# First attention: maxima one block of keys further ahead, weighting by the values in two halves

## The chip, the cores and the metric

The kernel runs on one core of one Trainium2 chip. The metric is the device time of one execution in microseconds (us), the median of several runs. The engines are called PE (TensorE, matrix products), DVE (VectorE), ACT (ScalarE), POOL (GpSimd) and SP (SyncE, which issues DMA transfers). PEld is PE's weight load, and an engine's name with a q (SPq) its sequencer.

## The reference

The input x has 2 batches of 2048 tokens with 256 features. Two residual blocks follow one another: an attention over all tokens, and a two-layer network with local attention. The change touches the first alone:

```
def _L0_attn_ref(x, Wq, bq, Wk, bk, Wv, bv, Wo, bo):
    q = _rope(proj(Wq, bq))        # 16 heads of 16 features, 2048 tokens
    k = _rope(proj(Wk, bk))
    v = proj(Wv, bv)
    scores = jnp.einsum('bhtd,bhsd->bhts', q, k) / scale
    attn = jax.nn.softmax(scores, axis=-1)
    out = jnp.einsum('bhts,bhsd->bhtd', attn, v)
    return jnp.einsum('btc,oc->bto', out, Wo) + bo

x = x + _layernorm(_L0_attn_ref(_layernorm(x, axis=-1), ...), axis=-1)
x = x + _layernorm(_L0_ffn_ref(_layernorm(x, axis=-1), ...), axis=-1)
```

## The kernel before

The program runs its phases one after the other: projection to queries, keys and values, `attention_phase`, output projection, feed-forward layers, and a final sum. All engines' orders are written out by hand, in one function per engine, and semaphores join them.

`attention_phase` handles 2 x 16 = 32 heads (NH) of 2048 tokens each. A head has 16 tiles (TB) of 128 tokens and 4 blocks (BLOCKS) of 512. A **step** is one tile of 128 keys of one head against the four blocks of 512 queries, so there are 512 steps. In a step

- PE makes four blocks of scores with `score` (L632), each into one of three banks `scores` (BANKS1). It waits until ACT has emptied the bank, which is done with the block of three blocks before.
- ACT makes the exponential of each block, with `exponentiate` (L696), into one of 12 slots of `probs` (three steps). At a step's first block it waits until PE has weighted the step three before (`pv_done`).
- PE weights the values with `weigh` (L644): four matmuls for the four blocks, each with a stationary operand of 32 columns at its own column position, into one bank `pv`, which accumulates over a head's 16 steps. In the trace each of these matmuls in full float32 has two records, so a call has eight.

The exponentials need each query's maximum over all keys beforehand. PE makes the scores again with queries as the stationary operand, in `for_dve` (L600), on another group of rows of the array than `score`, and DVE takes the maximum of two blocks at once with `take_maximum` (L729). Two blocks are a **unit** and lie in two banks of `aux`, of which there are two pairs; `unit_of` numbers the units. This runs ahead of the scores by AHEAD = 3 spans of 8 tiles, so the maxima of 24 tiles (OPENING) are made in an opening of their own, where ACT (L689) and DVE (L737) share the work. The queue of PE in the main loop is, for each block: `score`, then `for_dve` for the block 24 tiles ahead, and at block 1 of a step `weigh(step - 2)` behind them.

Once in a head the 16 x 128 maxima are transposed by PE (`maximum_rows`, L622, into a unit of `aux`), copied by DVE (`copy_rows`, L743), and sent by SP (`load_rows`, L488) to rows of `q_stack` for the scores of the next head. This sits at slot 13 of a head's second span, which is block 1 of step 11. When a head's weighting is complete, ACT copies `pv` to `o_stage` (`copy_outputs`, L704), at block 2 of the next head's step 1, and the next head's first `weigh` waits for the copy.

SP works through one list for each head n, and begins when PE raises `head_begun`, behind the score of block 1 of step 1: six loads of head n+1 for the scores, six loads of head n+2 for the maxima (both L482, from `qk_dram`), the inverse sums of head n-2, the outputs of head n-1 (L497, L498), the rows of head n+1 (L488), and the sums (L515, L503). The first maxima of a head wait for all six of its loads (`for_max_loaded`); its first score waits for its own six and for the rows.

Of the kernel before, what the change touches and what calls it, by code (L numbers as in the profile page):

```python
# [16 lines left out]
TB = T // P  # L17
# [345 lines left out]
BLOCKS = T // 512  # L363
BODY = 3
VW = 32
SPAN = TB // 2
SLOTS = SPAN * BLOCKS
SPANS = NH * TB // SPAN
AHEAD = 3
OPENING = AHEAD * SPAN  # L370
FIRST_ROWS = TB + 3
ROWS_SLOT = 13
PROBS = 3 * BLOCKS
BANKS1 = 3
LOADS = 6
# [24 lines left out]
def attention_phase(nc, qk_dram, sums_dram, VO, mask_sb, shift_sb, ident, load_output_weights):  # L400

    with ExitStack() as ctx:
# [32 lines left out]

        block = ctx.enter_context(nc.Block())

        WITH_MAXIMA = SPANS - AHEAD
        FIRST_ITEMS = 2 * OPENING
        Q_MINUS_PIECES = ((0, 0, 4), (0, 4, TB), (1, 0, SPAN))  # L440

        def item_of_exp(e):

            return FIRST_ITEMS + e

        def rows_here(p, i):

            return p % 2 == 1 and i == ROWS_SLOT and p // 2 + 1 < NH

        block_at = [divmod(i, BLOCKS) for i in range(SLOTS)]  # L450
        unit_of, rows_unit = {}, {}

        def count_units():

            unit = 0
            for t in range(OPENING):
                if t == FIRST_ROWS:
                    rows_unit[0] = unit
                    unit += 1
                unit_of[t, 0] = unit  # L460
                unit += 1
            for p in range(SPANS):
                for i in range(SLOTS):
                    if p < WITH_MAXIMA and block_at[i][1] % 2 == 1:
                        t, k = block_at[i]
                        unit_of[(p + AHEAD) * SPAN + t, k // 2] = unit
                        unit += 1
                    if rows_here(p, i):
                        assert block_at[i][1] % 2 == 1
                        rows_unit[p // 2 + 1] = unit  # L470
                        unit += 1

        count_units()
# [119 lines left out]
        def _(pe):  # L593
# [12 lines left out]
                    pe.wait_ge(act_emptied, item - BANKS1 + 1)  # L606
                return scores[:, item % BANKS1]

            def for_dve(t, keys):

                unit = unit_of[t, keys // 2]
                if keys % 2 == 0 and unit >= 2:
                    pe.wait_ge(dve_emptied, unit - 1)
                last = score_for_max(t, keys, aux[:, unit % 2, keys % 2])
                if keys % 2 == 1:
                    last.then_inc(dve_filled, 1)

            def maximum_rows(n):
# [13 lines left out]
                last = nc.tensor.matmul(out, k_stack[0:SCORE_ROWS, n % BODY, s * P:(s + 1) * P], q_stack[0:SCORE_ROWS, n % BODY, j * 512:(j + 1) * 512],  # L632
                                        start=True, stop=True).then_inc(act_filled, 1)

            def weigh(step):

                n, s = divmod(step, TB)
                if s == 0:
                    pe.wait_ge(v_made, n + 1)
                    if n:  # L640
                        pe.wait_ge(pv_copied, n)
                pe.wait_ge(act_emptied, item_of_exp(BLOCKS * (step + 1) - 1) + 1)
                for j in range(BLOCKS):
                    last = nc.tensor.matmul(pv[VW * j:VW * (j + 1)], v_ones[:, n % BODY, s, :], probs[:, (BLOCKS * step + j) % PROBS],  # L644
                                            start=(s == 0), stop=(s == TB - 1), skip_group_check=True, tile_position=(0, VW * j))
                last.then_inc(pv_done, 1)

            def first_difference(t, k):

                n, tile = divmod(t, TB)  # L650
                piece = [i for i, (head, start, stop) in enumerate(Q_MINUS_PIECES) if head == n and start <= tile < stop][0]
                pe.wait_ge(q_minus_made, piece + 1)
                pe.wait_ge(for_scores_loaded[n], 16 * LOADS)
                out, rows = for_act(2 * t + k), slice(0, SPLIT_ROWS)
                nc.tensor.matmul(out, q_stack[rows, n, tile * P:(tile + 1) * P], k_stack[rows, n, (2 + k) * 512:(3 + k) * 512], start=True, stop=False)
                for_dve(t, k)
                nc.tensor.matmul(out, q_minus_first[rows, t], k_stack[rows, n, k * 512:(k + 1) * 512], start=False, stop=True).then_inc(act_filled, 1)
                nc.tensor.matmul(pv[:], q_stack[max_rows, n, tile * P:(tile + 1) * P], k_stack[max_rows, n, k * 512:(k + 1) * 512], start=True, stop=True)

# [3 lines left out]
                for k in range(2):  # L663
                    first_difference(t, k)

            for p in range(SPANS):
                for i in range(SLOTS):
                    step, j = p * SPAN + i // BLOCKS, i % BLOCKS
                    score(p * SLOTS + i)
                    if i == 5 and p % 2 == 0:  # L670
                        nc.tensor.nop().then_inc(head_begun, 1)
                    if p < WITH_MAXIMA:
                        for_dve((p + AHEAD) * SPAN + block_at[i][0], block_at[i][1])
                    if rows_here(p, i):
                        maximum_rows(p // 2 + 1)
                    if j == 1 and step >= 2:
                        weigh(step - 2)
            weigh(NH * TB - 2)
            weigh(NH * TB - 1)

        @block.scalar
        def _(act):

            def positive_part(t, k, item):

                act.wait_ge(act_filled, item + 1)
                if t >= 2:
                    act.wait_ge(dve_emptied, unit_of[t - 2, 0] + 1)
                nc.scalar.activation(excess[:, t % 2, k], scores[:, item % BANKS1], ACT.Relu).then_inc(act_emptied, 1)  # L689

            def exponentiate(e):

                act.wait_ge(act_filled, item_of_exp(e) + 1)
                if e >= PROBS and e % BLOCKS == 0:
                    act.wait_ge(pv_done, (e - PROBS) // BLOCKS + 1)
                nc.scalar.activation(probs[:, e % PROBS], scores[:, item_of_exp(e) % BANKS1], ACT.Exp, scale=float(D1) ** -0.5).then_inc(act_emptied, 1)  # L696

            def copy_outputs(n):

                act.wait_ge(pv_done, TB * (n + 1))  # L700
                if n >= 2:
                    act.wait_ge(outputs_moved, 16 * BLOCKS * (n - 1))
                    act.wait_ge(sums_stored, 16 * BLOCKS * (n - 1))
                nc.scalar.copy(o_stage[:, n % 2], pv[:]).then_inc(pv_copied, 1)  # L704

            for t in range(OPENING):
                for k in range(2):
                    positive_part(t, k, 2 * t + k)
            for p in range(SPANS):
                for i in range(SLOTS):  # L710
                    if i == BLOCKS + 2 and p % 2 == 0 and p > 0:
                        copy_outputs(p // 2 - 1)
                    exponentiate(p * SLOTS + i)
            copy_outputs(NH - 1)

        @block.vector
        def _(dve):

            def larger_half(n):

                dve.wait_ge(dve_emptied, unit_of[(n + 1) * TB - 1, 1 if n else 0] + 1)
                nc.vector.tensor_tensor(head_max[:], mx[:, n % BODY, :, 0], mx[:, n % BODY, :, 1], ALU.max).then_inc(head_max_made, 1)  # L722

            def take_maximum(t, half):

                n, tile = divmod(t, TB)
                unit = unit_of[t, half]
                dve.wait_ge(dve_filled, unit + 1)
                nc.vector.tensor_reduce(mx[:, n % BODY, tile, half:half + 1], aux[:, unit % 2].rearrange("p a k -> p (a k)"), AX.X, ALU.max).then_inc(dve_emptied, 1)  # L729

            def take_joined_maximum(t, item):

                n, tile = divmod(t, TB)
                unit, above = unit_of[t, 0], excess[:, t % 2].rearrange("p a k -> p (a k)")
                dve.wait_ge(dve_filled, unit + 1)
                dve.wait_ge(act_emptied, item + 1)
                nc.vector.tensor_tensor_reduce(out=above, in0=aux[:, unit % 2].rearrange("p a k -> p (a k)"), in1=above, scale=1.0, scalar=LOWEST,  # L737
                                               op0=ALU.add, op1=ALU.max, accum_out=mx[:, n % BODY, tile, 0:1]).then_inc(dve_emptied, 1)
# [21 lines left out]
            for t in range(OPENING):  # L760
# [2 lines left out]
                take_joined_maximum(t, 2 * t + 1)  # L763
                if t == TB:
                    larger_half(0)
            for p in range(SPANS):
                n = p // 2
                for i in range(SLOTS):
                    if p < WITH_MAXIMA and block_at[i][1] % 2 == 1:
                        take_maximum((p + AHEAD) * SPAN + block_at[i][0], block_at[i][1] // 2)  # L770
                    if p % 2 == 1 and i == 3 and n + 1 < NH:
                        larger_half(n + 1)
                    if rows_here(p, i):
                        copy_rows(n + 1)
                    if p % 2 == 0 and i == 3 and n >= 2:
                        invert_sums(n - 2)
            invert_sums(NH - 2)
            invert_sums(NH - 1)
# [895 lines left out]
```

## Time and profile before

| | us |
|---|---|
| median of 3 runs | 3165.63 |
| lowest, highest | 3161.74, 3165.71 |
| the profiled execution, its own time | 3163.34 |
| its span in the profile | 3161.5 |
| the exponentials (L696) of attention, in the span | 204.4 to 1571.1 |

The span runs from the first to the last instruction that the profile shows; the execution's own time is 1.8 us longer. Busy time of PE is modelled, since matmuls are pipelined: a matmul's record is longer than the time for which it keeps the next from starting, and distances between starts say more than durations.

### The profile page before, as it was taken

How to read it: one execution, taken by the hardware profiler on the slowest of the kernel's cores; microseconds unless marked ns; L12 is line 12 of the kernel's file. 1: busy time of each engine (PE TensorE's matmuls, PEld its weight loads, DVE VectorE, ACT ScalarE, POOL GpSimd, SP SyncE). 2: the span in 40 equal slices, each digit the busy share in tenths (PEclk: the TensorE clock that was granted, in tenths of full speed). 3: DMA queues.
4: the chain of work that ended last, by engine and by line, in shares of the span. 5: the costliest groups of instructions: out<-in, count | busy, mean ns of one | idle time of the engine just before them, and what ended most of it. 6: DMA issues, size and time to landing. Idle time of an engine off the chain costs nothing. (4 is left out here: it accounts for less than half of the span.)

```text
span 3161.5 us, 53824 instructions
## 1 busy us (share of the span) xinstructions
PE 2882.8 (91%) x19416; PEld 1855.9 (59%) x19416; DVE 2401.8 (76%) x4758; ACT 2210.0 (70%) x4950; POOL 803.2 (25%) x992
## 2 busy tenths in 40 slices
PE   8599999999999999999857999999999999999995
PEld 7443333333333333333246887878888888887875
DVE  7478888888888888888156767777777777777774
ACT  5367777777777777777745766676667676767672
POOL 6500000000000000000074434434344344444432
PEclk9769999999999999999988999999999999999997
DMA  5603332333332233332050000000000000000002
GB/s 167 157 16 45 48 42 39 44 49 46 49 48 39 37 48 47 48 48 39 10 183 1 1 0 0 0 0 0 0 1 36 1 1 0 0 0 0 0 1 72
DMA packets 61724, 107.79 MB, mean 34 GB/s; under 512 B 29552, under 2 KB 41840, under 8 KB 54256
## 3 DMA queue, kind: packets, MB, share of 16 engines
q1 hardware_dynamic: 57008, 104.15, 17.8%
q8 instruction: 104, 1.70, 0.3%
q10 hardware_dynamic: 4544, 1.38, 0.2%
q14 instruction: 68, 0.56, 0.1%
HBM read 75.07 MB, written 25.69 MB: 32 GB/s over the span
## 5 line engine op out<-in xcount | busy, mean ns | idle before, releaser
L729 DVE TENSOR_REDUCE mx<-aux 128x1 f32<-128x1024 f32 x976 | 1153.4, 1218 | 142.3 <-PE aux L600 142.2
L696 ACT ACTIVATE probs<-scores 128x512 f32<-128x512 f32 x2048 | 1058.2, 603 | 287.4 <-PE scores L632 287.3
L600 PE MATMUL aux<-k_stack,q_stack 48*128 48x512 f32 x2000 | 806.3, 473 | 11.9 <-DVE mx L737 11.8
L632 PE MATMUL scores<-q_stack,k_stack 50*128 50x512 f32 x2048 | 748.5, 445 | 53.6 <-ACT probs L696 17.5
L632 PEld LDWEIGHTS scores<-q_stack,k_stack 50*128 50x128 f32 x2048 | 340.0, 185 | 670.2 <-ACT probs L696 646.3
L644 PE MATMUL pv<-probs,v_ones 128*32 128x512 f32 x4096 | 546.3, 605 | 0.0
L600 PEld LDWEIGHTS aux<-k_stack,q_stack 48*128 48x128 f32 x2000 | 338.2, 188 | 62.8 <-DVE mx L737 23.5
L569 POOL CAST m_parts<-head_max 128x16 fp32r<-128x16 f32 x32 | 6.3, 196 | 1276.7 <-DVE head_max L722 1276.7
L1267 PE MATMUL bank<-VO,w_sb 128*128 128x128 f32 x2816 | 328.7, 277 | 1.5 <-ACT VO L1354 1.5
L1267 PEld LDWEIGHTS bank<-VO,w_sb 128*128 128x128 f32 x2816 | 322.9, 194 | 2.5 <-ACT VO L1354 2.5
L1335 ACT ACTIVATE wqkv_sb<-wqkv_sb,wo_bo_sb 128x256 f32<-128x256 f32 (+1 forms) x512 | 250.5, 490 | 21.5 <-DVE wo_bo_sb L1438 12.7
L1438 DVE CUSTOM_DVE_ANT_0 wqkv_sb<-bank,mask_sb,wo_bo_sb 128x256 f32<-128x256 f32 (+1 forms) x512 | 212.5, 471 | 57.8 <-PE bank L1205 57.8
L1138 POOL TENSOR_SCALAR var_eps<-wo_bo_sb 128x1 f32<-128x1 f32 x64 | 31.9, 498 | 833.4 <-DVE wo_bo_sb L1483 833.4
L1368 ACT ACTIVATE wqkv_sb<-bank,b_sb 128x128 f32<-128x128 f32 x320 | 103.7, 365 | 147.0 <-PE bank L1267 147.0
L1216 PE MATMUL bank<-w_sb,wqkv_sb 128*128 128x256 f32 (+1 forms) x768 | 195.3, 396 | 2.3 <-DVE wqkv_sb L1427 1.7
L1538 DVE TENSOR_TENSOR VO<-bank,x_sb 128x256 f32<-128x256 f32 x64 | 27.2, 425 | 214.4 <-PE bank L1297 214.4
L1164 POOL TENSOR_TENSOR wo_bo_sb<-wo_bo_sb,minus_half 128x16 f32<-128x16 f32 x64 | 188.6, 2947 | 5.3
L1451 DVE TENSOR_TENSOR wqkv_sb<-wqkv_sb,wo_bo_sb 128x512 f32<-128x512 f32 (+1 forms) x256 | 182.9, 714 | 8.9
L1216 PEld LDWEIGHTS bank<-w_sb,wqkv_sb 128*128 128x128 f32 (+1 forms) x768 | 135.1, 189 | 57.4 <-issue 41.1
L1158 POOL TENSOR_TENSOR VO<-VO,wo_bo_sb 128x512 f32<-128x512 f32 x128 | 160.9, 1279 | 17.7 <-ACT VO L1345 17.4
L1241 PE MATMUL bank<-wqkv_hi,xT_hi 128*128 128x512 f32 x384 | 157.2, 410 | 5.4 <-DVE xT_lo L1467 4.0
L644 PEld LDWEIGHTS pv<-probs,v_ones 128*32 128x32 f32 x4096 | 80.6, 108 | 123.0 <-ACT probs L696 96.7
(178 smaller groups left out, 4655.0 us busy)
## 6 DMA issues: line engine op xcount, KB each, us to landing
q_stack<-qk_dram SPq DMA_DIRECT2D x192, 128.0 KB, 5.1
k_stack<-qk_dram SPq DMA_DIRECT2D x192, 128.0 KB, 6.9
qk_dram<-qkT_hi SPq DMA_DIRECT2D x32, 256.0 KB, 3.1
qk_dram<-qkT_lo SPq DMA_DIRECT2D x32, 256.0 KB, 3.6
VO<-o_stage SPq DMA_DIRECT2D x128, 32.0 KB, 7.1
inverse<-sums_dram SPq DMA_DIRECT2D x32, 128.0 KB, 3.0
out<-x_sb SPq DMA_DIRECT2D x9, 384.0 KB, 4.2
wqkv_sb<-in_wqkv SPq DMA_DIRECT2D x2, 1536.0 KB, 6.4
```

What stands on the lines that cost most here:

```text
L600: return nc.tensor.matmul(out, q_stack[max_rows, n % BODY, tile * P:(tile + 1) * P], k_stack[max_rows, n % BODY, keys * 512:(keys + 1) * 512],
L632: last = nc.tensor.matmul(out, k_stack[0:SCORE_ROWS, n % BODY, s * P:(s + 1) * P], q_stack[0:SCORE_ROWS, n % BODY, j * 512:(j + 1) * 512], ...
L644: last = nc.tensor.matmul(pv[VW * j:VW * (j + 1)], v_ones[:, n % BODY, s, :], probs[:, (BLOCKS * step + j) % PROBS], start=(s == 0), stop= ...
L696: nc.scalar.activation(probs[:, e % PROBS], scores[:, item_of_exp(e) % BANKS1], ACT.Exp, scale=float(D1) ** -0.5).then_inc(act_emptied, 1)
L729: nc.vector.tensor_reduce(mx[:, n % BODY, tile, half:half + 1], aux[:, unit % 2].rearrange("p a k -> p (a k)"), AX.X, ALU.max).then_inc(dv ...
L1158: nc.gpsimd.tensor_tensor(out=o4[:, :, :, lo:lo + D2 // 2], in0=q4[:, :, :, hi:hi + D2 // 2], in1=sin_table[:, st.table(2), :, lo:lo + D2 ...
L1164: nc.gpsimd.tensor_tensor(out=rnorm[:, st.slot(2, 2)], in0=norm2_min[:], in1=minus_half[:], op=ALU.pow).then_inc(sin_rnorm_made, 1)
L1216: last = nc.tensor.matmul(out[:, 0:C], act_T[rows, c], w2_sb[rows, st.layer(-1), c], start=(c == 0), stop=(c == HC - 1))
L1267: last = nc.tensor.matmul(out[:, i * P:(i + 1) * P], w1_sb[:, st.layer(0), k, chunk * P:(chunk + 1) * P], hT[:, k], start=(k == 0), stop=( ...
L1335: nc.scalar.activation(probs[:, j, u, keys], probs[:, j, u, keys], ACT.Exp, scale=-1.0, bias=negmax[:, j, u:u + 1], accum_out=sums[:, j, u ...
L1438: last = nc.vector.tensor_tensor_reduce(out=probs[:, j, u, at:at + n_keys], in0=src[:, 2 * u * P + at:2 * u * P + at + n_keys], in1=mask_s ...
L1451: nc.vector.tensor_tensor(p4, p4, rsums[:, j].unsqueeze(2).to_broadcast([P, 2, P * len(blocks)]), ALU.mult).then_inc(by_dve, 1)
```

## The change

- The lead of the maxima is counted in blocks. It goes from 24 tiles (96 blocks) to 21 tiles and one block, AHEAD = 85. The opening makes 21 tiles instead of 24, and one block's matmul of a 22nd ahead of the loop. Since 85 is odd, a unit is now opened at block 3 or 1 of a step and closed at block 0 or 2.
- `weigh` is split into halves of 256 columns. The second half of step - 2 follows block 0, and the first half of step - 1 follows block 2 (block 3 in step 1 of a head, where it waits for the copy).
- `head_begun` is raised at block 1 of step 5 instead of step 1. The transposed maxima move from block 1 of step 11 to block 2 of step 13. `larger_half`, which joins the two maxima of a query, moves from block 3 of step 8 to block 0 of step 11, `invert_sums` from block 3 of step 0 to block 0 of step 4, and `copy_outputs` from in front of block 2 of step 1 to in front of block 1.

```diff
-SPAN = TB // 2
-SLOTS = SPAN * BLOCKS
-SPANS = NH * TB // SPAN
-AHEAD = 3
-OPENING = AHEAD * SPAN
+HALF = 256
+STEPS = NH * TB
+LEAD = 5
+OPENING = TB + LEAD
+AHEAD = OPENING * BLOCKS + 1
-ROWS_SLOT = 13
+ROWS_STEP, LARGER_STEP = 13, 11
...
-            def weigh(step):
+            def weigh(step, half):
...
+                columns = slice(half * HALF, (half + 1) * HALF)
                 for j in range(BLOCKS):
-                    last = nc.tensor.matmul(pv[VW * j:VW * (j + 1)], v_ones[:, n % BODY, s, :], probs[:, (BLOCKS * step + j) % PROBS],
-                                            start=(s == 0), stop=(s == TB - 1), skip_group_check=True, tile_position=(0, VW * j))
-                last.then_inc(pv_done, 1)
+                    last = nc.tensor.matmul(pv[VW * j:VW * (j + 1), columns], v_ones[:, n % BODY, s, :], probs[:, (BLOCKS * step + j) % PROBS, columns],
+                                            start=(s == 0 and half == 0), stop=(s == TB - 1 and half == 1), skip_group_check=True, tile_position=(0, VW * j))
+                if half == 1:
+                    last.then_inc(pv_done, 1)
...
-            for p in range(SPANS):
-                for i in range(SLOTS):
-                    step, j = p * SPAN + i // BLOCKS, i % BLOCKS
-                    score(p * SLOTS + i)
-                    if i == 5 and p % 2 == 0:
+            for_dve(AHEAD - 1)
+            for step in range(STEPS):
+                for j in range(BLOCKS):
+                    score(BLOCKS * step + j)
+                    if (step % TB, j) == (LEAD, 1):
                         nc.tensor.nop().then_inc(head_begun, 1)
-                    if p < WITH_MAXIMA:
-                        for_dve((p + AHEAD) * SPAN + block_at[i][0], block_at[i][1])
-                    if rows_here(p, i):
-                        maximum_rows(p // 2 + 1)
-                    if j == 1 and step >= 2:
-                        weigh(step - 2)
-            weigh(NH * TB - 2)
-            weigh(NH * TB - 1)
+                    if BLOCKS * step + j + AHEAD < MAXIMA:
+                        for_dve(BLOCKS * step + j + AHEAD)
+                    if rows_here(step, j):
+                        maximum_rows(step // TB + 1)
+                    if j == 0 and step >= 2:
+                        weigh(step - 2, 1)
+                    if j == (3 if step % TB == 1 else 2) and step >= 1:
+                        weigh(step - 1, 0)
+            weigh(STEPS - 2, 1)
+            weigh(STEPS - 1, 0)
+            weigh(STEPS - 1, 1)
```

## Rows read from the trace of the kernel before

**Rows 1.** The page, busy tenths and PE's granted clock in 40 slices.

```profile
PE   8599999999999999999857999999999999999995
...
PEclk9769999999999999999988999999999999999997
```

**Rows 2.** Groups by line, 217 to 1507 us: busy, mean, idle before, releasers.

```profile
L696 ACT ACTIVATE probs<-scores 128x512 f32<-128x512 f32 x1935 | 999.6, 603 | 270.1 <-PE scores L632 270.1
...
L632 PEld LDWEIGHTS scores<-q_stack,k_stack 50*128 50x128 f32 x1932 | 319.4, 184 | 628.8 <-ACT probs L696 607.9
```

**Rows 3.** Timeline of one step: start, us, engine, line, operation, idle before.

```profile
1007.60 1.07 PE L644 MATMUL pv<-probs,v_ones 128*32 128x512 f32 x8
...
1008.05 0.61 PE L644 MATMUL pv<-probs,v_ones 128*32 128x512 f32 x4
...
1008.59 0.18 PEld L632 LDWEIGHTS scores<-q_stack,k_stack 50*128 50x128 f32 x1 [0.84 <-ACT probs L696]
...
1008.70 0.19 PEld L632 LDWEIGHTS scores<-q_stack,k_stack 50*128 50x128 f32 x1
...
1008.93 0.39 PE L600 MATMUL aux<-k_stack,q_stack 48*128 48x512 f32 x1
...
1009.12 2.06 ACT L696 ACTIVATE probs<-scores 128x512 f32<-128x512 f32 x4 [0.54 <-PE scores L632]
...
1009.16 0.39 PE L632 MATMUL scores<-q_stack,k_stack 50*128 50x512 f32 x1
...
1009.39 2.36 DVE L729 TENSOR_REDUCE mx<-aux 128x1 f32<-128x1024 f32 x2 [0.25 <-PE aux L600]
...
1009.77 0.18 PEld L632 LDWEIGHTS scores<-q_stack,k_stack 50*128 50x128 f32 x1 [0.39 <-ACT probs L696]
...
1010.20 0.16 PEld L644 LDWEIGHTS pv<-probs,v_ones 128*32 128x32 f32 x8 [0.24 <-ACT probs L696]
```

**Rows 4.** Timeline of ACT behind the last maxima.

```profile
1536.72 2.07 ACT L696 ACTIVATE probs<-scores 128x512 f32<-128x512 f32 x4 [0.54 <-PE scores L632]
1539.32 2.06 ACT L696 ACTIVATE probs<-scores 128x512 f32<-128x512 f32 x4 [0.54 <-PE scores L632]
```

**Rows 5.** Windows: length, busy (count) of PE, PEld, DVE, ACT, POOL, clock, DMA.

```profile
217.00:1507.00 1290.00, 1227.40 (x7768) 487.65 (x7766) 1150.20 (x1057) 1013.46 (x1965) 37.76 (x102) 1.00 0.32 44
...
2000.00:2010.00 10.00, 10.00 (x97) 9.28 (x97) 5.36 (x13) 5.29 (x13) 4.70 (x5) 1.00 0.00 0
```

**Rows 6.** Timeline of PE around the transposed maxima.

```profile
1001.60 1.07 PE L644 MATMUL pv<-probs,v_ones 128*32 128x512 f32 x8
...
1004.99 1.06 PE L644 MATMUL pv<-probs,v_ones 128*32 128x512 f32 x8
```

**Rows 7.** Timeline of SP: the first loads of three heads' lists.

```profile
1020.30 1.23 SPq L482 DMA_DIRECT2D q_stack<-qk_dram  x3
...
1063.00 1.23 SPq L482 DMA_DIRECT2D q_stack<-qk_dram  x3
...
1447.33 1.23 SPq L482 DMA_DIRECT2D q_stack<-qk_dram  x3
```

**Rows 8.** Line 482 at 1025.2 us: the last two loads of a head.

```profile
L482 SPq DMA_DIRECT2D k_stack<-qk_dram x2: 419/420/420, 1024.8 to 1025.3; - x2
...
DMA to landing us min/median/max: 9.4/9.7/10.0
```

**Rows 9.** Line 482 at 1452.2 us: the last two loads of another head.

```profile
L482 SPq DMA_DIRECT2D k_stack<-qk_dram x2: 420/420/420, 1451.8 to 1452.3; - x2
...
DMA to landing us min/median/max: 8.9/9.2/9.5
```

**Rows 10.** Line 488, the rows' 64 transfers: from issue to landing.

```profile
DMA to landing us min/median/max: 1.8/1.9/3.1
```

**Rows 11.** Timeline of ACT in the opening.

```profile
179.46 0.60 ACT L689 ACTIVATE excess<-scores 128x512 f32<-128x512 f32 x1 [0.28 <-PE scores L657]
...
183.21 0.60 ACT L689 ACTIVATE excess<-scores 128x512 f32<-128x512 f32 x1 [0.28 <-PE scores L657]
```

More of the change, by code:

```diff
@@ L436, in attention_phase, with rows_here @@
         block = ctx.enter_context(nc.Block())
-        WITH_MAXIMA = SPANS - AHEAD
+        MAXIMA = NH * TB * BLOCKS
         FIRST_ITEMS = 2 * OPENING
-        Q_MINUS_PIECES = ((0, 0, 4), (0, 4, TB), (1, 0, SPAN))
+        Q_MINUS_PIECES = ((0, 0, 4), (0, 4, TB), (1, 0, LEAD))
         def item_of_exp(e):
             return FIRST_ITEMS + e
-        def rows_here(p, i):
-            return p % 2 == 1 and i == ROWS_SLOT and p // 2 + 1 < NH
-        block_at = [divmod(i, BLOCKS) for i in range(SLOTS)]
+        def rows_here(step, j):
+            return step % TB == ROWS_STEP and j == 2 and step // TB + 1 < NH
         unit_of, rows_unit = {}, {}
@@ L459, in count_units @@
                     unit += 1
-                unit_of[t, 0] = unit
+                unit_of[t * BLOCKS] = unit_of[t * BLOCKS + 1] = unit
                 unit += 1
-            for p in range(SPANS):
-                for i in range(SLOTS):
[L464 to L467, printed above, removed]
-                    if rows_here(p, i):
-                        assert block_at[i][1] % 2 == 1
-                        rows_unit[p // 2 + 1] = unit
+            unit_of[AHEAD - 1] = unit
+            for step in range(STEPS):
+                for j in range(BLOCKS):
+                    m = BLOCKS * step + j + AHEAD
+                    if m < MAXIMA:
+                        unit_of[m] = unit
+                        unit += m % 2
+                    if rows_here(step, j):
+                        assert m % 2 == 1
+                        rows_unit[step // TB + 1] = unit
                         unit += 1
@@ L607, in for_act, with for_dve @@
                 return scores[:, item % BANKS1]
-            def for_dve(t, keys):
-                unit = unit_of[t, keys // 2]
-                if keys % 2 == 0 and unit >= 2:
+            def for_dve(m):
+                unit = unit_of[m]
+                if m % 2 == 0 and unit >= 2:
                     pe.wait_ge(dve_emptied, unit - 1)
-                last = score_for_max(t, keys, aux[:, unit % 2, keys % 2])
-                if keys % 2 == 1:
+                last = score_for_max(m // BLOCKS, m % BLOCKS, aux[:, unit % 2, m % 2])
+                if m % 2 == 1:
                     last.then_inc(dve_filled, 1)
@@ L633, in score @@
                                         start=True, stop=True).then_inc(act_filled, 1)
-            def weigh(step):
+            def weigh(step, half):
                 n, s = divmod(step, TB)
-                if s == 0:
+                if (s, half) == (0, 0):
                     pe.wait_ge(v_made, n + 1)
@@ L655, in first_difference @@
                 nc.tensor.matmul(out, q_stack[rows, n, tile * P:(tile + 1) * P], k_stack[rows, n, (2 + k) * 512:(3 + k) * 512], start=True, stop=False)
-                for_dve(t, k)
+                for_dve(t * BLOCKS + k)
                 nc.tensor.matmul(out, q_minus_first[rows, t], k_stack[rows, n, k * 512:(k + 1) * 512], start=False, stop=True).then_inc(act_filled, 1)
@@ L664, in _ @@
                     first_difference(t, k)
-            for p in range(SPANS):
-                for i in range(SLOTS):
-                    step, j = p * SPAN + i // BLOCKS, i % BLOCKS
-                    score(p * SLOTS + i)
-                    if i == 5 and p % 2 == 0:
-                        nc.tensor.nop().then_inc(head_begun, 1)
-                    if p < WITH_MAXIMA:
-                        for_dve((p + AHEAD) * SPAN + block_at[i][0], block_at[i][1])
-                    if rows_here(p, i):
-                        maximum_rows(p // 2 + 1)
-                    if j == 1 and step >= 2:
-                        weigh(step - 2)
-            weigh(NH * TB - 2)
-            weigh(NH * TB - 1)
+            for_dve(AHEAD - 1)
+            for step in range(STEPS):
+                for j in range(BLOCKS):
+                    score(BLOCKS * step + j)
+                    if (step % TB, j) == (LEAD, 1):
+                        nc.tensor.nop().then_inc(head_begun, 1)
+                    if BLOCKS * step + j + AHEAD < MAXIMA:
+                        for_dve(BLOCKS * step + j + AHEAD)
+                    if rows_here(step, j):
+                        maximum_rows(step // TB + 1)
[6 more added lines that the diff above has]
+            weigh(STEPS - 1, 1)
         @block.scalar
@@ L687, in positive_part @@
                 if t >= 2:
-                    act.wait_ge(dve_emptied, unit_of[t - 2, 0] + 1)
+                    act.wait_ge(dve_emptied, unit_of[(t - 2) * BLOCKS] + 1)
                 nc.scalar.activation(excess[:, t % 2, k], scores[:, item % BANKS1], ACT.Relu).then_inc(act_emptied, 1)
@@ L708, in _ @@
                     positive_part(t, k, 2 * t + k)
[L709 to L713, printed above, removed]
+            for step in range(STEPS):
+                for j in range(BLOCKS):
+                    if (step % TB, j) == (1, 1) and step > TB:
+                        copy_outputs(step // TB - 1)
+                    exponentiate(BLOCKS * step + j)
             copy_outputs(NH - 1)
@@ L719, in larger_half, with take_maximum @@
             def larger_half(n):
-                dve.wait_ge(dve_emptied, unit_of[(n + 1) * TB - 1, 1 if n else 0] + 1)
+                dve.wait_ge(dve_emptied, unit_of[(n + 1) * TB * BLOCKS - (1 if n else 3)] + 1)
                 nc.vector.tensor_tensor(head_max[:], mx[:, n % BODY, :, 0], mx[:, n % BODY, :, 1], ALU.max).then_inc(head_max_made, 1)
-            def take_maximum(t, half):
-                n, tile = divmod(t, TB)
-                unit = unit_of[t, half]
+            def take_maximum(m):
+                n, tile = divmod(m // BLOCKS, TB)
+                half, unit = m % BLOCKS // 2, unit_of[m]
                 dve.wait_ge(dve_filled, unit + 1)
@@ L733, in take_joined_maximum @@
                 n, tile = divmod(t, TB)
-                unit, above = unit_of[t, 0], excess[:, t % 2].rearrange("p a k -> p (a k)")
+                unit, above = unit_of[t * BLOCKS], excess[:, t % 2].rearrange("p a k -> p (a k)")
                 dve.wait_ge(dve_filled, unit + 1)
@@ L765, in _ @@
                     larger_half(0)
[L766 to L771, printed above, removed]
+            for step in range(STEPS):
+                n, s = divmod(step, TB)
+                for j in range(BLOCKS):
+                    m = BLOCKS * step + j + AHEAD
+                    if m < MAXIMA and m % 2 == 1:
+                        take_maximum(m)
+                    if (s, j) == (LARGER_STEP, 0) and n + 1 < NH:
                         larger_half(n + 1)
-                    if rows_here(p, i):
+                    if rows_here(step, j):
                         copy_rows(n + 1)
-                    if p % 2 == 0 and i == 3 and n >= 2:
+                    if (s, j) == (4, 0) and n >= 2:
                         invert_sums(n - 2)
```

## The prediction

> **What bounds the kernel now.** I read the page's 40 slices first [rows 1]: the stretch that the change touches (slices 3 to 19, at 79 us each) holds a 9 for PE throughout. A PE busy share is modelled, so I looked at that stretch alone, grouped by line [rows 2]. The reader is to see that both sides have idle time, and who ends it: the exponentials wait 270.1 us for PE, and PE's weight loads for scores wait 607.9 us for the exponentials. Engines that wait for each other form a loop of latencies, and none of them is full.
>
> The timeline of one step (a tile of 128 keys of a head against four blocks of 512 queries) shows the loop [rows 3]. The first score after the weighting is loaded at 1008.59 and its exponential starts at 1009.12 (0.53 later). The score three blocks on shares its bank and is loaded at 1009.77 (0.65 after that start). The weighting follows at 1010.20 (0.43), and a weighting holds the next score back by 0.99 (1007.60 to 1008.59). The sum is 2.60, and that is the period, from weighting to weighting (1007.60 to 1010.20). The check is the tail without maxima [rows 4]: with VectorE gone the exponentials still come in fours 2.60 to 2.61 apart. So neither reductions nor columns set the time, but the one long weighting between two scores that share a bank. Floors: VectorE 2 x 1.14 = 2.28 per step (two reductions take 2.36, one 1.22), ScalarE 4 x 0.49 = 1.95.
>
> **What the change does to a step.** Per step PE still issues four scores, four maxima blocks, and the same columns of weighting, but in two visits of 256 columns, each behind a pair that closes a unit. Price of a visit: the first four matmuls of the weighting start at 1007.60, the second four at 1008.05, the next score at 1008.59 [rows 3]. So the rounds are 0.45 apart, twice the 0.23 between two undisturbed pairs (1008.93 to 1009.16): such a matmul passes its 512 columns twice, 2 x 0.213 = 0.43 at 2.4 GHz (granted clock 1.00 [rows 5]). Halving the columns takes 0.21 off each round: 0.24 + 0.33 = 0.57 for a half visit. The trace has no half visit; bounds are 0.50 (all of it scales) and 0.99 (nothing does). I take 0.57, because the spacing of the rounds shows what scales.
>
> A visit costs its neighbours too. The first pair behind it has its weight load exposed: 1008.59 to the second load at 1008.70, 0.11, which makes 0.34 to the next pair. From the start of a pair's own matmul to a visit it is 0.43 - 0.11 = 0.32, against 0.23 to another pair. So half a step is 0.57 + 0.34 + 0.32 = 1.23 and a step 2.46, if nothing waits. Of this, fixed costs of switching are 2 x 0.35; the second 0.35 is what the split adds.
>
> Does anything wait? Score to the score that shares its bank: allowed after 0.53 + 0.65 = 1.18; in the new order a score and the third after it are at least 0.34 + 0.32 + 0.57 + 0.34 = 1.57 apart, so 0.39 to spare. Reduction: it starts 0.46 after its last matmul (1008.93 to 1009.39), ends 1.22 later, and the unit's banks are wanted 0.32 + 0.57 + 0.34 + 0.32 + 0.57 = 2.12 after that matmul, against 0.46 + 1.22 + 0.05 = 1.73: again 0.39 to spare. That is what the odd lead of maxima buys: a unit is closed just ahead of each visit, and VectorE reduces under it. VectorE needs 2.28 of 2.46. The third buffer of probabilities gives ScalarE a step of room (it waits for a weighting that PE issued over a step earlier). The loop of latencies is cut, and PE becomes the bound at 2.46.
>
> The Trainium skill speaks against the split: "TensorEngine Tiling (Array Packing)", Key Properties, says that changing the tiling mode drains TensorE, and scores, maxima and weighting use different modes. The 0.11 on either side of a visit agrees with it; without any drain a step would be 2 x 0.22 shorter and VectorE's 2.28 would bind; a drain dearer than these rows show is rival 2 below.
>
> Issue rate: a step now has 8 + 16 matmuls and as many loads, 48 in 2.46 us, 51 ns each. A later stretch sustains 97 + 97 in 10 us [rows 5], 52 ns each, without being shown to be at its limit. At exactly this rate a step would be 2.47; I add nothing.
>
> **Head boundaries.** Before, the step with the transposed maxima is 1001.60 to 1004.99, 3.39: 0.78 over [rows 6]. In the new order the maxima behind it open a unit in the banks of the unit just closed, which are free 1.73 after its closing matmul; the schedule had 0.32 + 0.57 = 0.89. So 0.84 after, 0.78 before. The copy of the outputs and a reciprocal stretch two more steps of a head, now by 0.16 together: a head is 42.70 (1020.30 to 1063.00 [rows 7]), and 16 x 2.61 + 0.78 leaves that. After, in the step with the copy the second visit moves from behind block 2 to behind block 3, since it must wait for the copy. The copy is done by then, but block 3's maxima come early and wait for the banks of their unit, free 1.73 after its closing matmul where they are due after 0.23 + 0.34 + 0.32 + 0.57 = 1.46, and their weight load is exposed: 0.27 + 0.11 = 0.38. The reciprocal fits in VectorE's slack.
>
> **What becomes late next: the loads.** The signal to SP moves from block 1 of step 1 to block 1 of step 5, and behind it stand 12 loads, then the store of inverses, the moved outputs and the rows. The maxima of head n+2 wait for all six of the second group of loads. They are due now at step 8: 6.75 steps of 2.61, 17.6 us after the signal. The loads need 15.0 us in one head (1020.30 to 1025.3 + 10.0) and 14.5 in another (1447.33 to 1452.3 + 9.5) [rows 7 to 9], so they are hidden. After, maxima run 85 blocks ahead, so head n+2 is due at block 3 of step 10: 22 blocks, 5.5 x 2.46 = 13.5 us after the signal. With 14.75 and 0.1 for two signals (an exponential's end is answered after 0.05 in [rows 3]) PE is short by 1.35 us (1.1 to 1.7), in front of the matmul that would open a unit, and nothing covers it since PE is the bound. This holds for the 29 heads 1 to 29; head 0 requests only the second group, and heads 30 and 31 have none due. The two transfers of the transposed maxima land 3.1 after their issue at most [rows 10]; a head had five steps for them, and now from step 13 to step 16, some 5.1 us after the copy. They fit.
>
> **Opening.** It loses 3 of 24 tiles. Their activations come four per 3.74 us (179.46 to 183.21 [rows 11]), 1.87 a tile: 5.6 us. Their maxima move under the main loop, which gets no step more. The page's clock digits are below full there [rows 1]; I assume that the loop's first steps see it as before.
>
> **Sum.** A head after: 16 x 2.456 + 0.84 + 0.38 + 1.35 = 41.87, gain 0.83; x 29 = 24.1. The three others gain 2.1 each: 6.3. Opening 5.6. In all 36.0. Against the profiled execution's own 3163.3 that is 3127.3; the median of the runs shown is 2.3 higher, so 3130. I forecast 3130.
>
> **Rivals.** (1) The loads are not late: they land sooner, or PE's queue, no longer stalled at each score, passes the signal well ahead of the array. Then 29 x 1.35 = 39 us more are gained: 3091. For it: a weighting's eight loads lie within 0.16 us (1010.20), while the second four matmuls start 0.45 late. Against: the landing is 14.5 and 15.0 whatever PE does, and running ahead is worth 0.4 a head at most, 3118. (2) Switching is dearer than priced, the one that ends slower. Since a longer step gives the loads more time, a head is 10.5 steps + 14.85 + 1.22; each 0.01 on the step costs 29 x 0.105 + 3 x 0.16 = 3.5 us, so 36 is used up at a step of 2.56: 0.05 us more per visit. At 0.08 more the step is 2.62 and the kernel near 3187. For it: PE has had a stall of 0.4 before each weighting in which to catch up; against: the costs on both sides are read from consecutive records. (3) The loads are late by twice as much, 2.7: they now meet the neighbours' traffic. 3130 + 39 = 3169, no change. Against: the moved outputs queue behind them, and the rows ahead of them are long landed. (4) The step stays 2.61, the exponentials binding by a path that I missed. The loads are then 0.53 late and the boundaries cost 0.30 more: 3166 - 6 + 29 x 0.83 = 3184. The 0.39 to spare on both loops speaks against it.
>
> **Numbers.** Forecast (with up to 12 us from running ahead) 0.58, rival 1 in full 0.12, rival 2 0.15 (two thirds of it slower by over 0.2%), rival 3 0.10, rival 4 0.05. A measurement of this kernel tells 0.2%, 6 us. Slower: 0.10 + 0.05 = 0.15. No change 0.10, most of rival 3 and some of rival 2. Faster: the rest, 0.75. The range takes in rival 1 and reaches to just below the kernel before, 3092 to 3163, leaving out most of rivals 2 and 4 and a part of 3; the forecast's own is 3115 to 3142.
>
> **What would show it.** Right: a reduction every 1.23 us with 0.09 idle before each, instead of a pair every 2.61; half visits of 0.57; a PE wait of about 1.3 us for a DMA at block 3 of step 10 of heads 1 to 29; opening 5.6 shorter. Wrong: half visits above 0.61, PE waits for exponentials in steady steps, or no wait for the loads.

## The result, and the profile after

The changed kernel takes 3112.92 us (median of 4 runs, 3103.96 to 3129.16) beside 3164.4 us of the kernel before in the same comparison: a ratio of 0.9845, 95% interval 0.9828 to 0.9861. It is faster by 1.5%. The forecast was 3130, in a range of 3092 to 3163. The measured time lies 2 us below the interval of 3115 to 3142 that the prediction gives its forecast alone. The profiled execution took 3114.72 us, 48.6 less than that of before; the forecast sum was 36.0 less. A spread of 25 us between runs is new: all runs of the kernel before, in all comparisons here, lie within 7 (3160.8 to 3167.2).

The page of the kernel after, its busy tenths and PE's granted clock:

```profile
PE   8599999999999999999758999999999999999995
...
DVE  7469999999999999998156777767777777777774
...
PEclk9759999999999999999879999999999999999998
```

A visit is one call of `weigh`, here of 256 columns, and a pair is a block of scores with the block of maxima that starts beside it. The timeline of PE in two halves of a step answers to [rows 3]:

```profile
1000.79 0.16 PEld L645 LDWEIGHTS pv<-probs,v_ones 128*32 128x32 f32 x8 [0.37 <-ACT probs L701]
1000.80 0.64 PE L645 MATMUL pv<-probs,v_ones 128*32 128x256 f32 x8
...
1001.36 0.18 PEld L632 LDWEIGHTS scores<-q_stack,k_stack 50*128 50x128 f32 x1 [0.41 <-ACT probs L701]
...
1001.70 0.39 PE L632 MATMUL scores<-q_stack,k_stack 50*128 50x512 f32 x1
...
1002.03 0.64 PE L645 MATMUL pv<-probs,v_ones 128*32 128x256 f32 x8
```

The timeline shows a half visit every 1.23 us (1000.80, 1002.03): from a visit to the next score 0.57, to the next pair 0.34 more, to the next visit 0.33 more. The idle times in brackets stand in front of weight loads and are no waits of the array: the "ACT" in them is the last semaphore that came, long before. A step is 2.467 us, where 2.456 was forecast and the kernel before had 2.61.

Behind the last maxima the visits stand in this way (timeline of PE):

```profile
1500.44 0.64 PE L645 MATMUL pv<-probs,v_ones 128*32 128x256 f32 x8
1501.67 0.64 PE L645 MATMUL pv<-probs,v_ones 128*32 128x256 f32 x8
1502.90 0.64 PE L645 MATMUL pv<-probs,v_ones 128*32 128x256 f32 x8
```

They are 1.23 apart there too, with no reductions left (a step is 2.45 instead of 2.467). So VectorE does not set the time, although in the steady steps a reduction's record begins within 0.01 us of the end of the last. PE does. The same stretch answers a question that the prediction left open, whether PE's rate of issue is the limit. At 48 matmuls and loads in 2.467 us the steady step has 51 ns for each, as forecast; without maxima a step has 40, and still takes 2.45, 61 ns each. The number of instructions does not set the time.

The head boundaries, as distances between visits (timeline of PE; first the transposed maxima, which answer to [rows 6], then the copy):

```profile
1021.80 0.64 PE L645 MATMUL pv<-probs,v_ones 128*32 128x256 f32 x8
1023.31 0.30 PE L622 MATMUL aux<-ident,m_parts 128*128 128x128 f32 x1 [0.21 <-DVE mx L734]
1023.54 0.64 PE L645 MATMUL pv<-probs,v_ones 128*32 128x256 f32 x8
1025.11 0.64 PE L645 MATMUL pv<-probs,v_ones 128*32 128x256 f32 x8
...
1032.51 0.64 PE L645 MATMUL pv<-probs,v_ones 128*32 128x256 f32 x8
1034.35 0.64 PE L645 MATMUL pv<-probs,v_ones 128*32 128x256 f32 x8
1035.34 0.64 PE L645 MATMUL pv<-probs,v_ones 128*32 128x256 f32 x8
```

The first two distances are 1.74 and 1.57, together 0.84 over 2 x 1.233; the last two are 1.84 and 0.99, together 0.37 over a step. Forecast were 0.84 and 0.38.

The loads: the timeline of SP and of PE's weight loads, and from the waits of 217 to 1500 us the row of a wait for a load (total, times, longest):

```profile
1001.88 1.23 SPq L482 DMA_DIRECT2D q_stack<-qk_dram  x3
...
1002.60 0.18 PEld L632 LDWEIGHTS scores<-q_stack,k_stack 50*128 50x128 f32 x1 [0.41 <-ACT probs L701]
```

```profile
PE aux L600 <- DMA k_stack<-qk_dram: 2.2, 6, 0.6
```

The list of SP begins at 1001.88, while the score in front of the signal (block 1 of step 5) is loaded at 1002.60. So PE's queue passes the signal 0.72 us before the array reaches that score, in each of heads 1 to 29. In the kernel before, SP begins 0.07 behind the same kind of score (1020.30 [rows 7], score at 1020.22), so the signal comes 0.8 earlier by its place in the queue. The loads themselves land as before, 14.7 us after the first issue on average in both kernels (14.2 to 15.2 in this one). The wait for them is therefore smaller than forecast. The row of waits undercounts it: from the starts of the exponentials, steps 10 and 11 of heads 1 to 30 last 2.64 and 2.81 on average, 0.52 over two steady ones.

The beginning of the loop, in windows of the kernel after (length; busy and count of PE, PEld, DVE, ACT, POOL; clock, DMA share, GB/s):

```profile
198.50:208.00 9.50, 8.91 (x39) 3.54 (x39) 7.18 (x7) 5.08 (x10) 0.00 (x0) 0.50 0.04 14
208.00:218.00 10.00, 10.00 (x60) 3.00 (x56) 5.76 (x5) 5.42 (x10) 0.00 (x0) 0.50 0.00 0
218.00:222.00 4.00, 4.00 (x28) 1.40 (x24) 2.13 (x3) 2.08 (x4) 0.00 (x0) 0.50 0.86 135
222.00:232.00 10.00, 10.00 (x100) 3.64 (x96) 9.58 (x9) 8.27 (x17) 0.00 (x0) 0.99 0.23 27
```

The first score starts at 198.5, 5.2 us earlier than before (203.7). The opening's first matmul came 0.6 later in this execution (146.9 against 146.2), so the opening itself is 5.9 shorter. But the clock is granted at half, 1.2 GHz, until 222. In the kernel before it came in full at 214, halfway through the second of these windows:

```profile
208.00:212.00 4.00, 3.82 (x17) 1.20 (x15) 3.83 (x4) 2.72 (x5) 0.00 (x0) 0.50 1.10 164
212.00:216.00 4.00, 4.00 (x24) 1.56 (x21) 2.18 (x3) 2.06 (x4) 0.00 (x0) 0.75 0.27 33
```

Steps 1 to 4 of the first head take 4.26, 4.38, 4.32 and 4.32 us; before, they took 2.53, 4.63, 2.60 and 2.61.

### The profile page after: what moved, and what is told of

The parts are those of the page before. It is cut to its first block and busy times, and to the rows that moved or that the text cites. A ratio compares the mean times of both kernels' runs of the same rounds, so it can differ in the third digit from the quotient of the medians.

```text
span 3112.9 us, 61971 instructions
## 1 busy us (share of the span) xinstructions
PE 2892.4 (93%) x23500; PEld 1831.6 (59%) x23500; DVE 2446.2 (79%) x4758; ACT 2257.7 (73%) x4944; POOL 802.3 (26%) x992
## 5 line engine op out<-in xcount | busy, mean ns | idle before, releaser
L701 ACT ACTIVATE probs<-scores 128x512 f32<-128x512 f32 x2048 | 1114.4, 596 | 199.1 <-PE scores L632 75.9
L734 DVE TENSOR_REDUCE mx<-aux 128x1 f32<-128x1024 f32 x982 | 1200.6, 1223 | 61.4 <-PE aux L600 53.7
L600 PE MATMUL aux<-k_stack,q_stack 48*128 48x512 f32 x2006 | 757.7, 453 | 16.1 <-DVE mx L742 10.8
L632 PE MATMUL scores<-q_stack,k_stack 50*128 50x512 f32 x2048 | 761.8, 450 | 0.0
L645 PE MATMUL pv<-probs,v_ones 128*32 128x256 f32 x8192 | 658.0, 393 | 0.1
L632 PEld LDWEIGHTS scores<-q_stack,k_stack 50*128 50x128 f32 x2048 | 310.2, 186 | 428.3 <-ACT probs L701 410.8
L645 PEld LDWEIGHTS pv<-probs,v_ones 128*32 128x32 f32 x8192 | 161.6, 108 | 361.0 <-ACT probs L701 290.6
L600 PEld LDWEIGHTS aux<-k_stack,q_stack 48*128 48x128 f32 x2006 | 306.8, 188 | 47.9 <-DVE mx L742 21.4
L1341 ACT ACTIVATE wqkv_sb<-wqkv_sb,wo_bo_sb 128x256 f32<-128x256 f32 (+1 forms) x512 | 250.4, 490 | 21.7 <-DVE wo_bo_sb L1444 12.8
```

Source lines behind the costliest of these rows:

```text
L600: return nc.tensor.matmul(out, q_stack[max_rows, n % BODY, tile * P:(tile + 1) * P], k_stack[max_rows, n % BODY, keys * 512:(keys + 1) * 512],
L645: last = nc.tensor.matmul(pv[VW * j:VW * (j + 1), columns], v_ones[:, n % BODY, s, :], probs[:, (BLOCKS * step + j) % PROBS, columns], sta ...
L1341: nc.scalar.activation(probs[:, j, u, keys], probs[:, j, u, keys], ACT.Exp, scale=-1.0, bias=negmax[:, j, u:u + 1], accum_out=sums[:, j, u ...
```

## The experiments

All edits are against the changed kernel. Steps are distances between the first exponentials of steps in the trace.

**Signal back at step 1.** Are the loads late, and does that cost what steps 10 and 11 show?

```diff
-                    if (step % TB, j) == (LEAD, 1):
+                    if (step % TB, j) == (1, 1):
```

> The changed kernel with the signal to SP for a head's loads back at block 1 of step 1; all else as changed. Theory A, the loads of a head land late for the maxima of the head after next: steps 10 and 11 of a head last 2.64 and 2.81 on average in the changed kernel, 0.42 more than 2.47 and the 2.57 that step 11 has in a head without this wait. Over 29 heads that is 12 us; with the signal four steps (9.9 us) earlier both go to 2.47 and 2.57, and the median goes from 3113 to 3101. Theory B, these steps are long because of the joining of the maxima on VectorE at step 11: they stay, and the median stays at 3113.

Measured: 3103.66 us (4 runs, 3092.79 to 3106.28), ratio to before 0.9801 (0.9777 to 0.9825). Steps 10 and 11 are 2.47 and 2.47 in every head, and a head takes 40.67 us each time (timeline of SP, first loads of three heads, 40.67 and 40.66 apart):

```profile
903.60 1.23 SPq L482 DMA_DIRECT2D q_stack<-qk_dram  x3
...
944.27 1.23 SPq L482 DMA_DIRECT2D q_stack<-qk_dram  x3
...
984.93 1.23 SPq L482 DMA_DIRECT2D q_stack<-qk_dram  x3
```

In the changed kernel heads took 40.66 to 41.71. Theory A holds, and even the 0.1 that I had put down to VectorE at step 11 was the loads: 0.52 x 29 = 15 us. The two profiled executions differ by 12.8 us (3114.72, 3101.95): the 15 of the loads, less 2.8 in the first head, where the clock stood at half for 6 us longer (until 228; steps 1 to 6 at 4.3). The medians differ by 9; the runs that were not profiled do not show how much of that is the clock.

**Signal a step later.** The same edit, with (6, 1).

> The changed kernel with the signal to SP one step later, at block 1 of step 6. Theory A, the loads' landing is on the path and nothing covers it: nearly the whole step of 2.47 us is lost in each of 29 heads, 65 to 72 us in all, about 3180, and it shows at steps 10 and 11. Theory B, the loads are hidden: no change from 3113.

Measured: 3467.51 us (one run). The waits of 230 to 1800 us, and the page's clock:

```profile
PE aux L600 <- DMA k_stack<-qk_dram: 70.8, 28, 3.3
```

```profile
PEclk9668867688776877898668899999999999999998
```

PE waits 70.8 us for the loads, 28 times, at the top of what theory A gave, so the loads are on the path. The kernel lost 354.6, though, where theory A forecast a loss of about 67. The rest is the clock. Behind 25 of the 28 waits (2.5 us on average, 3.3 at most; the three others are 1.8 to 2.0) it falls to half, for 10 to 72 us, and steps of 4.3 us follow (one head: 4.79, 4.32, 4.73, 4.32, 4.32 behind the wait, then 3.99 and full speed in the next head). From 230 to 1870 us the mean clock is 0.78, which is 710 us at half; at 4.32 for 2.467 a step that costs 305 us. The waits add 56 to the 15 of the changed kernel, and 361 is close to the loss. Neither theory had this. The changed kernel, with waits of 0.6 us at most, stands one step away from it.

**Even lead.** What is the one block more worth?

```diff
-AHEAD = OPENING * BLOCKS + 1
+AHEAD = OPENING * BLOCKS
...
-            return step % TB == ROWS_STEP and j == 2 and step // TB + 1 < NH
+            return step % TB == ROWS_STEP and j == 3 and step // TB + 1 < NH
...
-            unit_of[AHEAD - 1] = unit
...
-            for_dve(AHEAD - 1)
```

> The changed kernel with its halves and their places, but with the maxima 84 blocks ahead instead of 85, so that a unit is closed at block 1 or 3, just behind a half visit of weighting and not just ahead of it. Theory A, PE is the bound only because a unit is closed ahead of each visit: now the banks of a unit are wanted 1.46 us after its closing matmul and free after 1.73, so a step becomes 1.73 + 0.11 + 0.32 + 0.57 + 0.11 = 2.84 and the kernel takes 3113 + 490 x 0.37 - 12 (loads no longer late), about 3280. Theory B, the halves alone bring the gain and the place of the units matters little: 3113, steps 2.47.

Measured: 3336.98 us (one run), slower than the kernel before. The steady step is 2.84 to 2.85, as worked out. The timeline of PE's loads shows who stops it:

```profile
1000.20 0.16 PEld L644 LDWEIGHTS pv<-probs,v_ones 128*32 128x32 f32 x8 [0.26 <-issue]
...
1001.37 0.18 PEld L599 LDWEIGHTS aux<-k_stack,q_stack 48*128 48x128 f32 x1 [0.31 <-DVE mx L732]
1001.80 0.16 PEld L644 LDWEIGHTS pv<-probs,v_ones 128*32 128x32 f32 x8 [0.24 <-issue]
```

The load that opens a unit waits for VectorE at 1001.37, and the visits are 1.60 and 1.24 apart by turns (1000.20, 1001.80, 1003.04). The whole is 57 above the 3280 expected. The clock accounts for it: it falls ten times, always at step 14, behind the transposed maxima, for 157 us in all, and 4.32 for 2.84 a step makes 54 us of that (the page's clock digits go down to 8 in places). No wait of PE as long as those of the late signal stands in front of these falls: nine of the ten have none above 0.42 us in the 16 us before, the first 0.66. In this kernel the clock also came late at the start, 32 us after the first score. Theory B falls: halves at these places without the odd lead make a slower kernel. Not tried is the even lead with the visits moved to behind blocks 1 and 3, where each would again follow a pair that closes a unit. So it is shown that the visits need such a pair ahead of them, and not that the lead must be odd.

**Joined visits.** What is the odd lead worth without the halves?

```diff
                     if j == 0 and step >= 2:
+                        weigh(step - 2, 0)
                         weigh(step - 2, 1)
-                    if j == (3 if step % TB == 1 else 2) and step >= 1:
-                        weigh(step - 1, 0)
+            weigh(STEPS - 2, 0)
```

> The changed kernel with the odd lead kept, but both halves of step - 2 back to back behind block 0, one visit per step. Theory A, the gain comes from cutting the loop score, exponential, score with the whole weighting in it: the loop is back, a step is 2.61, and the time is that of before or a little more, 3165 to 3185. Theory B, the odd lead alone brings the gain (VectorE gets its unit in time): steps near 2.47 and about 3113; or, since PE spends 0.35 less per step on switching, even 2.28.

Measured: 3168.75 us (one run), 3 us above the kernel before (3165.99, median of 7). The exponentials come in fours again, 2.61 apart, with the same idle time as in [rows 3] (timeline of ScalarE):

```profile
1001.32 2.06 ACT L701 ACTIVATE probs<-scores 128x512 f32<-128x512 f32 x4 [0.54 <-PE scores L632]
1003.93 2.06 ACT L701 ACTIVATE probs<-scores 128x512 f32<-128x512 f32 x4 [0.54 <-PE scores L632]
```

Theory A holds. The loop of score, exponential and score with the whole weighting inside is what the split cuts. Neither edit gains anything without the other at these places of the visits. A side result: in this kernel the clock was granted in full 10 us after the first score, as before the change.

**Joined visits at the start only.** That side result, tried by itself in the changed kernel.

```diff
+JOINED = 8
...
                     if j == 0 and step >= 2:
+                        if step <= JOINED:
+                            weigh(step - 2, 0)
                         weigh(step - 2, 1)
-                    if j == (3 if step % TB == 1 else 2) and step >= 1:
+                    if j == (3 if step % TB == 1 else 2) and step >= JOINED:
                         weigh(step - 1, 0)
```

> The changed kernel, but in steps 2 to 8 of the first head both halves follow block 0 in one visit; from then on as changed. Theory A, half visits with their drains keep TensorE's clock at 1.2 GHz longer at the start of the main loop: it was granted in full 24 us after the first score in the changed kernel, 30 in the one with the early signal, but 10 in the kernel before and in the one with joined visits. Now it is 10 again, the first six steps take 17.7 instead of 24.0 us, and the median goes from 3113 to about 3106, with a smaller spread than 3104 to 3129. Theory B, the clock is released by the passing of time or by the loads' end: it stays at 24 to 30 us, and the median at 3113.

Measured: 3108.08 us (4 runs, 3106.42 to 3117.39), ratio 0.9834 (0.9819 to 0.9849). The clock is full from 207, 10 us after the first score at 197, and the first head takes 43.76 us instead of 49.50. Theory A holds for the clock, and the spread is 11 us instead of 25. In the median the gain is 5 us, and the interval overlaps that of the changed kernel, so for the time alone the comparison does not settle it.

**Both.** The early signal and the joined start together.

> The changed kernel with the signal to SP at block 1 of step 1 and the joined visits in steps 2 to 8 of the first head. Theory A: both gains add. Heads of 40.67 us, clock in full 10 us after the first score, 3103.7 - 8 (the kernel with the early signal lost 28.7 us to its first six steps and a half more) = 3090 to 3097. Theory B, the clock does not depend on the visits: 3103.

Measured: 3092.77 us (5 runs, 3090.99 to 3095.70), ratio 0.9779 (0.9765 to 0.9792). Theory A holds: the time lies within its 3090 to 3097. The heads take 40.67 us, the first one 43.84, and the spread is 5 us again. It is the fastest kernel here, 20 us under the changed one, and the intervals are apart. Its windows at the start and in the loop:

```profile
196.90:206.50 9.60, 9.01 (x41) 3.98 (x41) 7.16 (x8) 5.60 (x12) 0.00 (x0) 0.50 0.59 94
206.50:216.50 10.00, 9.83 (x98) 4.91 (x96) 9.36 (x8) 7.79 (x17) 0.00 (x0) 0.99 0.01 2
217.00:1480.00 1263.00, 1256.61 (x11915) 470.45 (x11915) 1193.70 (x1062) 1091.69 (x2021) 40.67 (x112) 1.00 0.32 46
```

**Quarters.** Is the price of a visit what the argument says?

```diff
-HALF = 256
+HALF = 128
...
-                if half == 1:
+                if half == 3:
                     last.then_inc(pv_done, 1)
...
-                    if (step % TB, j) == (LEAD, 1):
+                    if (step % TB, j) == (1, 1):
...
-                    if j == 0 and step >= 2:
-                        weigh(step - 2, 1)
-                    if j == (3 if step % TB == 1 else 2) and step >= 1:
-                        weigh(step - 1, 0)
+                    if j < 2 and step >= 2:
+                        weigh(step - 2, 2 + j)
+                    if j >= 2 and step >= 1:
+                        weigh(step - 1, j - 2)
...
```

> The changed kernel with the weighting in four visits of 128 columns a step, one behind each block, and the signal at block 1 of step 1. Theory A, a visit costs PE its columns and a fixed 0.35 (drain in and out, two exposed weight loads), and PE is the bound: 2.47 + 2 x 0.34 = 3.15 a step, which the reductions (2.28) and the exponentials (1.95) do not touch, about 3104 + 350 = 3450, more if the clock falls. Theory B, VectorE is the bound of the changed kernel (its reductions stand 1.23 apart with under 0.01 idle): a step stays near 2.47 as long as PE keeps up.

Measured: 4490.6 us (one run). The first half of the loop in a window:

```profile
200.00:1500.00 1300.00, 1299.04 (x9840) 485.16 (x9844) 611.28 (x540) 594.18 (x1003) 16.32 (x49) 0.50 0.16 23
```

The clock is granted at half for the whole attention, although PE's records cover 1299.04 of 1300 us. Every steady step is 5.23. The linear price holds at this clock: a step streams 4 x 512 columns for the pairs, and for the weighting two rounds of 512 at two passes, 2048; together 4096 / 1.2 GHz = 3.41 us; two visits gave 4.32 (0.45 each over the columns), and four would be 3.41 + 4 x 0.45 = 5.23. At full clock two visits give 2.467 - 1.71 = 0.76, 0.38 each, so four would be 3.23, a figure that no run shows. Between theory A and theory B this run does not decide, since at half clock PE is slower than VectorE's 2.28 in any case; what speaks against B is the stretch without maxima above, where the visits keep their distance. Theory A's 3450 was out by 1040. The clock is the reason: 512 steps at 5.23 and not at the estimated 3.23 are 1024 us. Whether these visits would hold the full clock if they began at it, no run shows.

## Why the prediction was right

The time fell in the range and on the forecast's side, and the terms can be read one by one. The mechanism that carries the gain, a loop of latencies that the split cuts, is what the runs show.

- **The bound before.** The loop of latencies (2.60 from its four parts) was right: keeping everything but the split brings back 2.61 (joined visits).
- **The step.** 2.456 forecast, 2.467 measured; over 512 steps that is 6 us too little. The half visit was 0.57 as worked out from the spacing of the rounds. Of the signs named, the reduction every 1.23 us came; the 0.09 idle before each did not, since a reduction's record is 1.22 long, although two can start 1.14 apart, as in [rows 3]. The 0.09 is room and not idle time in the trace.
- **The odd lead.** That a unit "is closed just ahead of each visit" was the right reason: with the even lead the same recurrence gives 2.84, and 2.84 was measured.
- **Boundaries.** 0.84 and 0.38 forecast, 0.84 and 0.37 measured.
- **The loads.** The mechanism was right, its size was not: 1.35 a head forecast, 0.52 measured, 24 us over 29 heads. The step that was off is "running ahead is worth 0.4 a head at most": the signal comes 0.8 earlier than at the same place before, and that is nearly all of the 0.83 by which the wait was too dear. The landing was as forecast, 14.7 beside 14.75. Rival 1 was half true, and the forecast's own sign, a wait of 1.3 in each head, did not come.
- **The opening.** Three tiles less saved 5.9 us where 5.6 was forecast; the first score is only 5.2 earlier because the opening began 0.6 later in this execution.
- **The clock.** "I assume that the loop's first steps see it as before" was wrong. Half visits held TensorE at 1.2 GHz for 24 us of the loop instead of 10. The first head took 49.5 us, where the sum has that of before, 44.75, less 2.1: 6.9 us lost.

The sum of these is 36.0 - 6 + 24 - 7 = 47, beside 48.6 measured. The loads were priced 24 too dear, the step and the clock 13 too cheap. The two errors have opposite signs, and that part of the forecast's nearness is luck: had the step and the clock come as forecast, the time would have been some 13 us lower still.

As to the rule of the Trainium skill that a change of tiling mode drains TensorE ("TensorEngine Tiling (Array Packing)", Key Properties): the runs fit it and do not show the drain by itself. A visit costs 0.38 us beside its columns at full clock and 0.45 at half, where four visits a step cost the same each as two. How much of that is a drain and how much the exposed weight loads, no run separates. The prediction counts three modes, but a score and its maxima start together (1001.37 both), so these two run side by side and only the weighting can call for a change.

What stays open: why the array's clock comes later with half visits, of which the runs show only that it does; and why one execution of the changed kernel took 3129. Its mean clock was lower (0.963, against 0.969 to 0.973 in the others), which fits either a longer stretch at half clock at the start or a fall as in the experiments with the late signal and the even lead, but that execution was not profiled.

## What to carry to other kernels

When one engine feeds two others through few buffers, look for the longest uninterruptible piece of its work inside the loop of latencies: here splitting it paid only together with a place at which the other engine's buffers were not yet due, and either edit alone was worth nothing or less. Price the split by its fixed costs (here 0.38 us a visit) and count what becomes due earlier, the transfers above all. And do not price a wait of TensorE by its own length alone: look at the granted clock behind it. Here a kernel with 71 us of waiting, 56 more than its neighbour, was 355 us slower.

## What the runs showed of the hardware

- PE can be covered by its own records for 1299 of 1300 us and still be granted half its clock, all the time, with four visits of 128 columns a step between pairs of 512. With two visits of 256 columns a step the clock came 24 to 32 us after the first score, in four kernels; with one visit of the same columns it came after 10, in all four kernels in which visits were whole or joined at the start.
- Once full, the clock stayed full at two visits a step over 1300 us in the changed kernel, whose longest wait of PE was 0.6. It fell behind 25 of 28 waits of 1.7 to 3.3 us (late signal), for 10 to 72 us each. With the even lead it fell ten times behind waits of 0.4 to 0.7 us, for 3 to 31 us each, while with joined visits at the start only it stayed full behind waits of up to 0.9. So the length of a wait alone does not tell whether it falls.
- PE's queue executes an empty instruction's signal before the array reaches the matmul in front of it: SP begins on it 0.72 us before that matmul in the changed kernel, and 0.07 behind it in the kernel before, where PE waits in front of its scores (0.39 there).
